# A two-layer graph network: the middle table keeps centred rows beside their inverse roots

## The reference, cut to what matters

```python
# x: 100000 x 64, 25000 edges, dst sorted, src random
x = layernorm(x + L0(x, src, dst, edge_attr_16))       # attention over edges, projection, ELU, layer norm
x = layernorm(x + L1(x, src, dst, edge_attr_3))
# L1 ("target" = dst, "source" = src):
d      = gelu(ln(gelu(ln(coords @ Wd1 + bd1)) @ Wd2 + bd2))      # per edge
logits = (x @ W1)[target] - (x @ W2)[source] + d
a      = segment_softmax(logits, target)
out    = segment_sum(a * ((x @ W3)[source] + d), target)
```

## Time and profile before

| | us |
|---|---|
| median of 3 runs (lowest, highest) | 1679.94 (1673.39, 1681.29) |
| the profiled execution | 1682.82 |
| its span, first to last instruction | 1680.9 |
| busy: PE, DVE, ACT, POOL | 1199.9, 1273.6, 852.7, 1037.9 |
| mean granted TensorE clock | 0.865 of full |

### The profile page before, as it was taken

The page is one execution under the profiler, slowest core; times in us unless marked ns, Lnnn a source line. Parts: engine busy times, 40 slices in busy tenths (PEclk is TensorE's granted clock), DMA queues, the critical chain, the costliest instruction groups (busy, mean ns, idle before and its releaser), DMA issues. The chain is left out here.

```text
span 1680.9 us, 19947 instructions
## 1 busy us (share of the span) xinstructions
PE 1199.9 (71%) x5229; PEld 753.8 (45%) x5253; DVE 1273.6 (76%) x2492; ACT 852.7 (51%) x1806; POOL 1037.9 (62%) x1043
## 2 busy tenths in 40 slices
PE   5888888888888830089999985267777766667762
PEld 4666665665665610024444443144444444444431
DVE  2999999999999959859999996146666666666673
ACT  1878877877878820024444441144444444444441
POOL 2777777777777700004777677554777777777755
PEclk9999999999999965579999996568887778888786
DMA  2556556665556540011222121022222222223210
GB/s 83 164 182 194 182 179 197 192 191 186 182 181 202 155 145 0 3 27 34 59 53 59 52 57 46 14 57 53 64 65 55 59 62 67 67 67 93 54 39 22
DMA packets 162060, 161.41 MB, mean 96 GB/s; under 512 B 82994, under 2 KB 99681, under 8 KB 161948
## 3 DMA queue, kind: packets, MB, share of 16 engines
q1 hardware_dynamic: 130300, 130.40, 25.0%
q0 software_dynamic: 31648, 29.74, 8.2%
HBM read 66.78 MB, written 82.77 MB: 89 GB/s over the span
## 5 line engine op out<-in xcount | busy, mean ns | idle before, releaser
L465 POOL DMA_INDIRECT dense_pairs<-in_x_dram,gix x392 | 405.1, 1033 | 181.6 <-issue 125.8
L1437 POOL DMA_INDIRECT out_dram<-second_orow,last_rows x196 | 207.3, 1058 | 105.8 <-issue 56.1
L1431 POOL DMA_INDIRECT second_sources<-x_table,gix x196 | 205.6, 1049 | 70.8 <-issue 59.5
L1011 POOL DMA_INDIRECT x_table<-first_xr,first_stage x200 | 205.3, 1026 | 54.3 <-issue 51.7
L491 PE MATMUL twin<-AC,dense_hb 128*128 128x256 f32 x784 | 194.2, 391 | 60.0 <-DVE dense_hb L643 60.0
L491 PEld LDWEIGHTS twin<-AC,dense_hb 128*128 128x128 f32 x784 | 142.0, 191 | 89.7 <-DVE dense_hb L643 74.1
L1005 POOL COPY first_stage<-first_rows 128x4 int32<-128x4 int32 x50 | 10.1, 201 | 210.9 <-POOLq L718 131.4
L483 PE MATMUL bank<-dense_xT,Mblk 128*128 128x512 f32 x196 | 107.0, 628 | 11.4 <-ACT dense_xT L579 11.4
L499 PE MATMUL bank<-prm,dense_xT 128*128 128x128 f32 x784 | 106.3, 278 | 5.4 <-DVE dense_yc L687 2.2
L1058 PE MATMUL twin<-first_zb,Mhead 128*128 128x512 f32 x200 | 109.7, 634 | 0.1
L1527 PE MATMUL twin<-Wd,second_ea 7*128 7x128 f32 x200 | 49.4, 422 | 75.6 <-ACT XT L1667 74.8
(11 more groups left out here) (337 smaller groups left out, 3171.0 us busy)
## 6 DMA issues: line engine op xcount, KB each, us to landing
dense_rows<-in_x_dram SPq DMA_DIRECT2D x98, 256.0 KB, 3.5
x_table<-dense_xr SPq DMA_DIRECT2D x98, 256.0 KB
out_dram<-dense_orow SPq DMA_DIRECT2D x98, 256.0 KB
XT<-dense_turned SPq DMA_DIRECT2D x50, 256.0 KB, 2.6
target_rows<-first_xr SPq DMA_DIRECT2D x50, 128.0 KB, 2.5
dense_pairs<-in_x_dram,gix POOLq DMA_INDIRECT x392
second_targets<-target_rows SPq DMA_DIRECT2D x49, 128.0 KB, 2.5
first_mask<-mask_rows SPq DMA_DIRECT2D x50, 64.0 KB
```

Source lines behind the costliest of these rows:

```text
L465: pool.indirect_dma_start(out=pairs[b][:, j % 4, F * (j // 4):F * (j // 4) + F], out_offset=None, in_=x, in_offset=bass.IndirectOffsetOnAx ...
L1011: pool.indirect_dma_start(out=x1, out_offset=bass.IndirectOffsetOnAxis(ap=stage[b][:, 4 * s + j:4 * s + j + 1], axis=0), in_=xr[b][:, 2 * ...
L1431: pool.indirect_dma_start(out=sources[u.off % 3][:, j, F * s:F * s + F], out_offset=None, in_=x1, in_offset=bass.IndirectOffsetOnAxis(ap=g ...
L1437: pool.indirect_dma_start(out=out, out_offset=bass.IndirectOffsetOnAxis(ap=last_rows[:, at:at + 1], axis=0), in_=orow[u.off % 4][:, 2 * j ...
```

## The change

The table `x1` gets rows of 65 numbers: 64 of the centred row and its inverse root. In dense, `finish` no longer multiplies for the table; it copies 8 roots a partition into the 65th column of `yc`, and SP stores `yc` itself. In first, finished rows are scattered with a 1.0 in the 65th column. In second, POOL gathers 65 numbers into new buffers `raw`, DVE multiplies them into `sources` (`scale_rows`) as the last work of a slot, and PE turns them as the last work of its slot.

```diff
-    x1 = nc.dram_tensor("x1_table", [N, F], fp32, kind="Internal").ap()
+    x1 = nc.dram_tensor("x1_table", [N, F + 1], fp32, kind="Internal").ap()
 # dense, SP and DVE
-                    sp.dma_start(node_rows(x1, u), xr[b][:, :, :].rearrange("p r f -> p (r f)")).then_inc(stored[b], 16)
+                    sp.dma_start(node_rows(x1, u), yc[u.off % 4][:, :, :].rearrange("p r f -> p (r f)")).then_inc(stored[b], 16)
                 def finish(u):
                     dve.wait_ge(roots_made, u.count(3))
                     atleast(dve, stored[b], u.halves(0) * 32)
-                    nc.vector.tensor_tensor(xr[b][:, :, :], yc[u.off % 4][:, :, :],
-                                            w[b][:, 8:16].unsqueeze(2).to_broadcast([128, 8, F]), ALU.mult)
+                    nc.vector.tensor_copy(yc[u.off % 4][:, :, F:F + 1], w[b][:, 8:16].unsqueeze(2))
                 def add_scaled(u):
-                    atleast(dve, out_made, u.count(-3))
+                    atleast(dve, stored[u.off % 2], u.halves(-1) * 32)
 # first, DVE (xr has 65 columns, the last set to 1.0 once)
-                    nc.vector.tensor_tensor(xr[b][:, :, :], yc[b][:, :, :],
+                    nc.vector.tensor_tensor(xr[b][:, :, 0:F], yc[b][:, :, :],
 # second, POOL
-                        out=sources[u.off % 3][:, j, F * s:F * s + F], out_offset=None, in_=x1,
+                        out=raw[u.off % 3][:, 2 * j + s, :], out_offset=None, in_=x1,
 # second, PE
                 def turn_lead():
-                    pe.wait_ge(lead_in, 16)
+                    pe.wait_ge(cleared, 11)
                 def turn(u):
-                    pe.wait_ge(gathered[b], arrived(u, 64))
+                    pe.wait_ge(rows_scaled, u.count(1))
                     pe.wait_ge(targets_in[b], arrived(u, 16))
                 def slot(u):
                         falls(u)
-                    if u.off == -1:
-                        turn_lead()
-                    if u.back(-1).valid(STEPS):
-                        turn(u.back(-1))
                     if u.valid(STEPS):
                         turn_denominators(u)
 ...
                         last.then_inc(rows_made, 1)
+                    if u.off == -1:
+                        turn_lead()
+                    if u.back(-1).valid(STEPS):
+                        turn(u.back(-1))
 # second, DVE
                 def start_targets():
+                    dve.wait_ge(lead_in, 16)
+                    nc.vector.tensor_tensor(lead[:, F:2 * F], lead[:, F:2 * F], lead[:, 2 * F:2 * F + 1].to_broadcast([128, F]),
+                                            ALU.mult).then_inc(cleared, 1)
                     dve.wait_ge(lead_turned, 1)
+                def scale_rows(u):
+                    b = u.off % 3
+                    dve.wait_ge(gathered[b], arrived(u, 64))
+                    atleast(dve, turned, u.count(-2))
+                    nc.vector.tensor_tensor(by_halves(sources[b]), raw[b][:, :, 0:F],
+                                            raw[b][:, :, F:F + 1].to_broadcast([128, 8, F]), ALU.mult).then_inc(rows_scaled, 1)
                 def slot(u):
                     if u.off == 0:
                         number_tail()
                         start_targets()
+                        scale_rows(u)
 ...
                         scale(a)
+                    if u.off >= 0 and u.back(-1).valid(STEPS):
+                        scale_rows(u.back(-1))
```

More of the change, by code:

```diff
@@ L349, in gnn @@
             yb = sbp("yb", [128, 8, F])
-            yc = [sbp(f"yc{i}", [128, 8, F]) for i in range(4)]
+            yc = [sbp(f"yc{i}", [128, 8, F + 1]) for i in range(4)]
             q2 = [sbp(f"q2{i}", [128, 8, F]) for i in range(2)]
@@ L938, in gnn @@
             yc = [sbp(f"yc{i}", [128, 8, F]) for i in range(2)]
-            xr = [sbp(f"xr{i}", [128, 8, F]) for i in range(2)]
+            xr = [sbp(f"xr{i}", [128, 8, F + 1]) for i in range(2)]
             s2 = sbp("s2", [128, 8])
@@ L1249, in slot @@
                         nc.vector.memset(v[:, :], 1.0)
+                        for b in range(2):
+                            nc.vector.memset(xr[b][:, :, F:F + 1], 1.0)
                         nc.vector.memset(start[:, :], 0.0).then_inc(cleared, 1)
@@ L1291, in gnn @@
             sbp, semp = places(ph, "second")
+            raw = [sbp(f"raw{i}", [128, 8, F + 1]) for i in range(3)]
             sources = [sbp(f"sources{i}", [128, 4, 2 * F]) for i in range(3)]
@@ L1321, in gnn @@
             marks = sbp("marks", [128, 128], bf16)
-            lead = sbp("lead", [128, 128])
+            lead = sbp("lead", [128, 2 * F + 1])
             every = sbp("every", [128, 128])
@@ L1342, in gnn @@
             (turned, copied, held, linear, topped, carried, fell_made, below_made, exps_made, term_made, summed,
-             rows_made, inverse_steps, off_made, quo_made, over_made, res_made, total_made, cen_made, sqr_made,
+             rows_made, inverse_steps, rows_scaled, quo_made, over_made, res_made, total_made, cen_made, sqr_made,
              s2_made, root_steps, gap_made, roots_made, out_made, cleared) = (
@@ L1455, in slot @@
                         pool.indirect_dma_start(
-                            out=lead[:, F:2 * F], out_offset=None, in_=x1,
+                            out=lead[:, F:2 * F + 1], out_offset=None, in_=x1,
                             in_offset=bass.IndirectOffsetOnAxis(ap=gix[:, 8 * UPPER + 4:8 * UPPER + 5], axis=0))\
```

31 lines of the change are left out of this document (17 added, 14 removed).

## The result

The changed kernel took 1733.25 us (median of 4 runs, 1731.98 to 1736.26); the kernel before, beside it on the same chip, took 1680.62. The ratio is 1.032, with a 95% interval of 1.029 to 1.035: slower by 53 us, where 49 had been forecast. The span of the profiled execution is 1734.4 us (before 1680.9).

The account below looks back on a forecast made before the run. DVE was taken to pace dense, and a chain round the engines to bound second. Terms -38 + 0 + 82 + 5 = +49 us on 1682.8 gave 1731.8, forecast as 1729; 8 in 10 for 1700 to 1765.

Parts of the forecast that it names:

- Dense, -38: Dense: DVE swaps a product for a small copy, gaining 0.53 us in three of four slots; -38 us, bounds -53 to -19.
- Wide rows, 0: Table stores and gathers with rows of 260 bytes: any dearer transfers stay hidden, costed at 0.
- A step, 3.1 to 4.1, taken as 3.5: Each step of second: the turn waits for DVE's product, so copy and gelus start later; 20 steps of 3.5 us make 70.
- the ring: Second: a chain that goes round from engine to engine once a step, 22.20 us each, with no engine near full.
- The first step, 2.8: First step of second, without roots of a step before: about +2.8 us for scale_rows and the turn.
- The last three steps, 9: End of second, where gelus run out: 3.3 + 3.3 + 2.5 = 9 us longer.
- Start of second, +5: Start of second: the first turn waits for the lead's work and step 0's scale_rows, so L1527 starts 5 us later.
- A: Rival, second: PE gets 2.4 GHz through distances and logits, shortening the chain; about 1656 us in total, chance 0.08.
- B: Rival, second: PE idles mid-step too and its work outside the logits runs at 1.2 GHz; 1774 us, chance 0.08.
- C: Rival: 260-byte rows make stores or descriptors dearer, dense loses its gain, scatters and gathers lengthen; 1772 us, chance 0.08.
- D: Low end of the forecast: larger cover, or full dense gain with the turn at the higher clock; 1705, within the forecast's 0.76.
- The signs: What would show it right: dense slots about 4.95 us, maxima 25 to 26.5 apart, copy waiting 3 or more, POOL standing longer.

Follow-up runs that it names:

- multiply-early kernel: Changed kernel with DVE's product ahead of the maxima and PE's turn back at its old place: 1644.22 us, ratio 0.977; on a longer chip 1923.67 us, 1.002.
- turn-late kernel: Kernel before with only PE's turn moved to the end of its slot: 1731.53 us, ratio 1.029; on a longer chip 1803.51 us, 0.942.
- dense-product: Changed kernel with dense multiplying whole rows for the table again: 1844.86 us, ratio 0.965, and 1849.04 us, 0.975, on two longer chips.

## Why the prediction was right

It was right in its direction and nearly in its size (1729 against 1733), by its own steps. Term by term the errors are +1.8, -2.7, +3.0, +3.3, -0.4 and -0.2 us (dense, twenty steps, first step, last three, start, tail); that they leave less than 5 together is in part luck:

- **Dense, -38** (the sum as written gives -39). It measured -36.3 at the start of second; dense itself ends 36.9 earlier (574.1 for 611.0). The instructions of first, forecast at 0, span 430.6 us for 431.0. The count of three slots of four held: the slots without logits are 0.43 to 0.53 us shorter, the fourth is a chain over PE and ScalarE, now with 1.38 us of idle time on DVE, for 0.88. The copy was priced at 0.08 and delays by 0.06. The end of four slots came 0.1 us later than worked out. DVE is no longer nearly full, so a further cut there would be worth less.
- **Wide rows, 0.** True for the time: the multiply-early kernel has them and steps like the kernel before, and dense gained what the count of slots gives. On POOL, gathers and scatters take 1.04 and 1.03 us in the kernel after, for 1.07. The gathered rows did cost transfer time, which had room. The queue of the gathers and scatters (packets, MB, share of 16 engines) in twenty steps before, 443.94 us, and after, 511.29 us:

```profile
q0 software_dynamic: 9888, 9.05, 9.4%
...
q0 software_dynamic: 10028, 9.28, 9.3%
```

Summed over the 16 DMA engines, that is 33 us a step before and 38 after, some 15% more for 2.5% more bytes. It is 38 with wide rows and 33 with narrow ones in the multiply-early and the turn-late kernel too, and in the dense-product and the turn-late kernel on the first longer chip; on the last longer chip it is only 34 with wide rows (changed kernel). The Trainium skill, "DMA: Bandwidth & Descriptors", section "How a descriptor splits into AXI transactions", has a descriptor that doesn't start on a 256-byte boundary start its first transaction at the boundary below, where the unused bytes still cost beats (of 32 bytes). That the gathers got dearer agrees with it; that the alignment is the reason was not shown. No cost of it shows in dense: a DMA share of 0.66 at 205 GB/s, nearly in proportion to 0.61 at 193.

- **A step, 3.1 to 4.1, taken as 3.5.** Twenty steps grew by 67 us, 3.37 each, where 70 were forecast. The mechanism is as worked out: L1763 behind L1869, then the turn, then the copy. The split was off, and the errors cancelled: the turn ran at the higher clock (1.10 us), so the ring's own part is 3.03, just under the low end; and the stretch from the distances to the maxima, which I had left alone, became 0.33 and 0.42 us longer. The idle stretch ahead of the turn, which the prediction took as 2.7 us, was 0.88 and 1.06, since the numerators end only at 12.05 and 11.87. So the turn was no burst behind a long wait, and the rule by the Trainium skill's "TensorE: Matmul & The Clock Gate" (section "HAM oscillation — how this bites in real kernels") on bursts that alternate with waits, by which I had weighed 4.0, is not tested by it. The distances do stand behind a long wait (3.44 us) and run at the lower level in every step, 2.07 us; there the trace agrees.
- **One thing the prediction left out**: it read the new place of the turn only by VectorE's product. In TensorE's own order the turn stands behind the numerators, which end 12.05 us behind the maxima; that alone is worth 1.7 to 1.8 a step (turn-late kernel), at the clock which the numerators get there. The product's end at about 12.9 covers it, so the sum was unhurt, but an early product with the turn still late would by these rows keep 1.7 to 1.8 of the loss.
- **The first step, 2.8, measured 5.8.** By share this is the term that was mis-sized most. The turn-late kernel has the same 5.8 without any product: in this step there are no roots ahead of the copy, so before, the gelus waited only for the numerators (10.40 us behind the maxima) and the distances ran at the higher clock (1.24 us). Now the gelus start at 14.84, 4.4 later, and the distances take 2.07.
- **The last three steps, 9, measured 12.3** (24.03, 22.29 and 21.43 for 20.01, 18.62 and 16.80): the last one lost 4.6 for 2.5. In its share of that, the exponents already start 5.83 us behind the maxima for 4.14; I did not follow that further.
- **Start of second, +5**, measured +4.6.
- **The rivals.** A (the clock turns the ring round) would have shown distances of about 1 us; they are 2.07 in each step, and the granted clock went down, from 0.81 to 0.73. B had the sign of the clock right and its size wrong: 0.4 us a step, not 1.2, and none for the turn. C is out, as above. D's dense in full did not come (36 of 53). (A's range was also added up wrongly: with -53 in dense its terms give 1645, not 1650.)
- **The signs.** Dense slots of 4.96 to 5.06 and maxima 25.0 to 26.2 apart are as named; the copy waits 2.92 us for L1506, a little under the 3 that were named; POOL stands 111.3 us for the finished rows of 166 transfers, before 30.0 for 162.

## What to carry to other kernels

When an operation moves on one engine, look at both things that will then hold it: what it waits for, and what now stands ahead of it in its own engine's order; here the place alone cost 1.8 us, and the wait brought it to 3.0. A product that is needed a step later belongs into the stretch where its engine waits for the ring, not to the end of the slot: with the same instructions, that placement, and with it the turn back in its early place, turned +53 us into -37 on chips where the kernel before takes 1681. And rank kernels on more than one chip: the same two kernels, changed and before, stood at 1.032 on one chip and at 0.994 on another.

## What the runs showed of the hardware that I had not expected

- **Stands without a cause in the profile.** On three of four chips ScalarE stood up to 25 us, mostly behind a table load, in nearly every second step, in the kernels whose ScalarE has no wait ahead of that load; in those with the copy behind the gelus VectorE stands too (10.44 us above). Those in which ScalarE waits 1.7 to 2.9 us for the late turn ran their last stage at the length that it has where the kernel before takes 1681, to within 0.6 us (566.2 for 566.5; 602.8 to 603.5 for 603.3). The dense stage, where VectorE and TensorE stand in this way, ended at 654 to 672 us on those chips in every kernel, in place of 574 or 611. What differs between the chips, and whether it is that wait which protects, is open: no run here separates them.
- **A level that isn't where the idle time is.** In the changed kernel's step above the numerators ran at the lower level (granted clock 0.50 from 1329.90 to 1331.80), and the turn, 0.88 us behind them, at the higher one (1.00 from 1332.69 to 1333.80; 0.66 and 0.60 us for four transposes each). The stretch from the distances to the maxima, whose matmuls had not moved against each other, became 0.33 to 0.42 us longer. The one does not follow from the other: in the turn-late kernel the turn got the higher level too (0.60 and 0.60), and that stretch takes 7.65 us, for 7.22 and 8.27 before.
- **Rows of 260 bytes.** With them the queue of the gathers and scatters took about 15% more transfer time than with rows of 256, on two chips, and no step got longer by it.
